# Seven of GpSimd's 392 gathers become single-row fetches that SyncE issues from a loaded address

## The chip, the cores and the metric

The kernel runs on one core of one Trainium2 chip. Times are device microseconds (us) of one execution, and the lower the better. A core has TensorE (PE: matmuls, with PEld its weight loads), VectorE (DVE), ScalarE (ACT), GpSimd (POOL) and SyncE (SP), each with an instruction queue of its own. [...] Transfers are carried by 16 DMA engines, whichever queue issues them.

## What is computed

One graph layer with a pre-norm over 100000 nodes of 64 features and 25000 edges:

```
h = jnp.maximum(_layernorm(x, axis=-1), 0.0)
x_i = h[src]; x_j = h[dst]
z = jnp.concatenate([x_i, x_j, edge_attr_32], axis=-1)
e = jax.nn.sigmoid(z @ W_f + b_f) * jax.nn.softplus(z @ W_s + b_s)
message = jax.ops.segment_sum(e, src, num_segments=100000)
normed = (message - mean) * jax.lax.rsqrt(var + BN_EPS) * gamma + beta
out = x + h + normed
```

So 2 x 25000 rows of x, 256 bytes each, have to be fetched by index, and 25000 message rows have to be added to a table by index.

## The kernel before

The work has two stages. Stage one gathers, computes the messages, and adds them to the table `msgs` in HBM; beside that it normalises all nodes into `y_kept` (the first 19 groups of it are spilled to HBM). Stage two squares the table for its variance, scales it, adds `y` and writes the output. A barrier of all engines stands between the stages, at about 900 us.

**Groups.** An edge group is 4 tiles of 128 edges; there are 49 (n = 0 to 48). For each tile GpSimd issues two gathers of 128 rows (`c` = 0 for source, 1 for destination), so a group has 8 gathers into `xg[:, n % 6, 2 * j + c, :]`, a ring of six slots (`gather`, L371 to L381). After gather(n) GpSimd issues the four scatters of group n - 6 (`accumulate`, L383 to L394), which wait for that group's combined messages (`comb_copied`), its targets, and the landing of the scatters before. GpSimd's program is a flat list; gather(n) waits only until group n - 6 has been centred.

**The other engines** run a pipeline of steps, one step for each group. Step n of VectorE ends the messages of group n - 3 (L545), sums and centres 16 node rows per partition (L459, L450), then waits for the gathers of group n, sums them (L470) and centres them (L450), which frees the slot; it normalises the group before (L519), makes targets, adds the residual of the group before (L537, four parts, the last of which raises `y_done`), and ends with `softplus` (L512). ScalarE and TensorE take squares, turns, products and the combination of equal sources between these.

**SyncE** loads the plain inputs. After a start with constants and the zeroing of `msgs` it runs a loop of 7 rounds (it = 1 to 7), six groups a round (u = 0 to 5), and in each group `load` issues 512 KB of x (`load_nodes`, L297 to L306) and the edge attributes (L308 to L320). `load(Group(it, u))` waits for `y_done` of group 6 it + u - 3 and for `ea_turned`. Thus in the loop SyncE loads two groups ahead of VectorE. The loop and its neighbours are:

```
            with sp.Fori(1, ITERS) as it:
                for u in range(UNROLL):
                    load(Group(it, u))
            for u in range(GROUPS - LAST + SKEW):
                load(Group(ITERS, u))
```

Of the kernel before, what the change touches and what calls it, by code (L numbers as in the profile page):

```python
# [21 lines left out]
I32 = mybir.dt.int32  # L22
ALU = mybir.AluOpType
# [3 lines left out]
P = 128  # L27
NODES, EDGES, F, EF = 100000, 25000, 64, 32
EPS = 1e-5
TILES = 4  # L30
GATHERED = 2 * TILES
# [4 lines left out]
ALL_TILES = E_COLS + 1  # L36
# [5 lines left out]
UNROLL = 6  # L42
# [4 lines left out]
G_SLOTS = 6  # L47
# [2 lines left out]
ACC_LAG = 6  # L50
ZERO_PARTS = 16
DUMP = (TILES + 1) * P
assert ALL_TILES == TILES * GROUPS and ITERS * UNROLL == LAST and UNROLL % SLOTS == 0 and UNROLL % G_SLOTS == 0
assert 0 < LAST_ROWS < BULK
assert (SPILL + 1 + SKEW) % UNROLL == 0
# [58 lines left out]
def wait_group(eng, sem, g, per=1):  # L114

    if not g.known or g.n >= 0:
        eng.wait_ge(sem, per * (g.n + 1) if per > 1 else g.n + 1)
# [43 lines left out]
def stage_one(nc, sem, x, src, dst, ea, w_f, b_f, w_s, b_s, msgs, y_spill,  # L161
              x_rows, ea_tiles, m_rows, y_kept, ones, ident, eps_col, one_col, msg_sum):
    with ExitStack() as ctx:
        def sb(name, shape, dt=F32):
            return ctx.enter_context(nc.sbuf_tensor(name, shape, dt))
# [1 line left out]
        def ps(name, shape):  # L167
            return ctx.enter_context(nc.psum_tensor(name, shape, F32))

        ids = sb("ids", [P, 2, ALL_TILES], I32)  # L170
        src_f = sb("src_f", [P, ALL_TILES])
        dump_row = sb("dump_row", [P, TILES])
        small = sb("small", [P, 4])
# [15 lines left out]
        xg = sb("xg", [P, G_SLOTS, GATHERED, F])  # L189
# [38 lines left out]
        prep = sem("prep")  # L228
# [2 lines left out]
        x_loaded = [sem(f"x_loaded{i}") for i in range(SLOTS)]  # L231
        ea_loaded = [sem(f"ea_loaded{i}") for i in range(SLOTS)]
        gathered = [sem(f"gathered{i}") for i in range(G_SLOTS)]
        own_staged = sem("own_staged")
        nodes_summed = sem("nodes_summed")
        edges_summed = sem("edges_summed")
        centred = sem("centred")
# [37 lines left out]
        def _(sp):  # L275
# [20 lines left out]
            def load_nodes(g):  # L296
                slot = g.slot(SLOTS)  # L297
                wait_group(sp, y_done, g.back(SLOTS))
                if g.known and g.n == STEPS - 1:
                    sp.dma_start(xn[:, slot, 0:LAST_ROWS, :],  # L300
                                 x_rows[:, BULK * LAST:N_ROWS, :]).then_inc(x_loaded[slot], 16)
                    sp.dma_start(xn[0:N_REST, slot, LAST_ROWS, :],
                                 x[P * N_ROWS:NODES, :]).then_inc(x_loaded[slot], 16)
                else:
                    sp.dma_start(xn[:, slot, :, :],
                                 x_rows[:, bass.ds((g.n - SKEW) * BULK, BULK), :]).then_inc(x_loaded[slot], 16)  # L306

            def load_edges(g):  # L308
                slot = g.slot(SLOTS)
                wait_group(sp, ea_turned, g.back(SLOTS))  # L310
                if g.known and g.n == LAST:
                    sp.dma_start(eas[:, slot, 0:TILES - 1, :],
                                 ea_tiles[:, E_COLS - TILES + 1:E_COLS, :]).then_inc(ea_loaded[slot], 16)
                    sp.dma_start(eas[0:E_REST, slot, TILES - 1, :],
                                 ea[P * E_COLS:EDGES, :]).then_inc(ea_loaded[slot], 16)
                    sp.dma_start(eas[E_REST:P, slot, TILES - 1, :],
                                 ea[0:P - E_REST, :]).then_inc(ea_loaded[slot], 16)
                else:
                    sp.dma_start(eas[:, slot, :, :],
                                 ea_tiles[:, bass.ds(g.n * TILES, TILES), :]).then_inc(ea_loaded[slot], 16)  # L320

            def load(g):
                if g.nodes():
                    load_nodes(g)
                if g.exists():
                    load_edges(g)
# [3 lines left out]
            def zero_table(u):  # L330
# [5 lines left out]
                if u == ZERO_PARTS - 1:  # L336
                    sp.dma_start(m_rows[:, whole:N_ROWS, :],
                                  zeros[:, 0:(N_ROWS - whole) * F].rearrange("p (r f) -> p r f", f=F)
                                  ).then_inc(table_zeroed, 16)
                    over = (N_REST + DUMP) // 96  # L340
                    sp.dma_start(msgs[P * N_ROWS:NODES + DUMP, :].rearrange("(p r) f -> p (r f)", p=96),
                                  zeros[0:96, 0:over * F]).then_inc(table_zeroed, 16)
# [5 lines left out]
            for u in range(SLOTS, UNROLL + 1):  # L348
                end = ZERO_PARTS * (u - 1) // (UNROLL - 1) if u < UNROLL else ZERO_PARTS
                for k in range(done, end):  # L350
                    zero_table(k)
                done = end
                if u < UNROLL:
                    load(Group(0, u))
            with sp.Fori(1, ITERS) as it:
                for u in range(UNROLL):
                    load(Group(it, u))
            for u in range(GROUPS - LAST + SKEW):
                load(Group(ITERS, u))

        @block.gpsimd
        def _(pool):
            pool.sem_inc(slots_free, UNROLL - 1)

            pool.memset(ident[:, :], 0.0).then_inc(masks_set, 1)
            pool.memset(upto[:, :], 1.0).then_inc(masks_set, 1)
            pool.wait_ge(masks_set, 2)
            pool.affine_select(out=ident[:, :], in_=ident[:, :], compare_op=ALU.not_equal, fill=1.0,
                               base=0, pattern=[[-1, P]], channel_multiplier=1).then_inc(masks_made, 1)
            pool.affine_select(out=upto[:, :], in_=upto[:, :], compare_op=ALU.is_ge, fill=0.0,  # L370
                               base=0, pattern=[[-1, P]], channel_multiplier=1).then_inc(masks_made, 1)  # L371

            def gather(n):
                if n >= G_SLOTS:
                    pool.wait_ge(centred, n - G_SLOTS + 1)
                for j in range(TILES):
                    for c in range(2):
                        pool.indirect_dma_start(  # L378
                            xg[:, n % G_SLOTS, 2 * j + c, :], None, x,
                            bass.IndirectOffsetOnAxis(ap=ids[:, c, n * TILES + j:n * TILES + j + 1], axis=0),  # L380
                        ).then_inc(gathered[n % G_SLOTS], 16)  # L381

            def accumulate(n):  # L383
                pool.wait_ge(comb_copied, n + 1)
                pool.wait_ge(target_done, n + 1)

                if n:
                    pool.wait_ge(accumulated, 16 * TILES * n)
                pool.sem_inc(slots_free, 1)
                for j in range(TILES):  # L390
                    pool.indirect_dma_start(  # L391
                        msgs, bass.IndirectOffsetOnAxis(ap=target[:, n % UNROLL, j:j + 1], axis=0),
                        comb[:, n % UNROLL, j, :], None, compute_op=ALU.add,
                    ).then_inc(accumulated, 16)  # L394

            pool.wait_ge(ids_loaded, 96)
            for n in range(GROUPS + ACC_LAG):
                if n < GROUPS:
                    gather(n)
                if n == ACC_LAG:  # L400
                    pool.wait_ge(table_zeroed, 16 * (ZERO_PARTS + 2))
                if n >= ACC_LAG:
                    accumulate(n - ACC_LAG)
            pool.wait_ge(accumulated, 16 * ALL_TILES)

        @block.vector
        def _(dve):
            dve.memset(zeros[:, :], 0.0).then_inc(zeros_set, 1)
            dve.memset(w_e[:, :, :], 0.0).then_inc(w_cleared, 1)
            dve.wait_ge(ids_loaded, 96)  # L410
            dve.memset(ones[:, :], 1.0)
            dve.memset(one_col[:, :], 1.0)
# [7 lines left out]

            dve.tensor_scalar(small[:, 1:2], small[:, 0:1], float(E_REST) + 0.5, None, ALU.is_lt)
            dve.tensor_scalar(small[:, 2:3], small[:, 0:1], float(NODES + TILES * P - 1), None, ALU.add)
            dve.tensor_copy(src_f[:, :], ids[:, 0, :]).then_inc(prep, 1)
            dve.wait_ge(prep, 2)
            dve.tensor_scalar(real[:, :], ones[:, :], small[:, 1:2], None, ALU.mult)
            dve.tensor_tensor(small[:, 3:4], src_f[:, E_COLS:ALL_TILES], small[:, 2:3],
# [21 lines left out]
            def less_mean(g, rows, x_of):  # L448
                n = rows.stop - rows.start
                return dve.scalar_tensor_tensor(  # L450
                    out=xc[:, g.slot(2), rows, :], in0=row_sum[:, rows].unsqueeze(2).to_broadcast([P, n, F]),
                    scalar=-1.0 / F, in1=x_of, op0=ALU.mult, op1=ALU.add)
# [12 lines left out]

            def centre_edges(g):
                slot, rows = g.slot(G_SLOTS), slice(0, GATHERED)
                dve.wait_ge(gathered[slot], 16 * GATHERED * g.uses(G_SLOTS) + 16 * GATHERED)
                wait_group(dve, centred, g.back(1))
                dve.tensor_reduce(row_sum[:, rows], xg[:, slot, :, :], AX.X, ALU.add).then_inc(edges_summed, 1)  # L470
                wait_group(dve, edges_summed, g)
                wait_group(dve, z_turned, g.back(2))
                less_mean(g, rows, xg[:, slot, :, :]).then_inc(centred, 1)

            def sum_squares(g):
                wait_group(dve, squared, g)
# [614 lines left out]
```

## Time and profile before

| | us |
|---|---|
| time, median of 3 runs (lowest, highest) | 1121.86 (1121.76, 1122.15) |
| the profiled execution: its own time | 1120.95 |
| its span in the trace | 1119.0 |
| busy: GpSimd, VectorE, TensorE, ScalarE | 684.3, 712.6, 703.5, 487.6 |
| stage one, up to the first load of stage two | 900.5 |

The span is 1.95 us shorter than the time of the same execution. Indices of lines are those of the kernel before. SyncE computes nothing, and its rows show when it issues transfers ("SPq"). Where a row has a bracket, it holds the time for which the engine stood idle before the instruction, and what ended that.

### The profile page before, as it was taken

The page shows a single profiled execution, that of the slowest core. Times are in us where ns is not written, and L with a number is a line of the kernel's source. Part 1 is how long each engine was busy: PE and PEld are TensorE (multiplying, and loading weights), DVE is VectorE, ACT ScalarE, POOL GpSimd, SP SyncE. Part 2 cuts the span into 40 slices and gives each one's busy share as a digit, 9 for nine tenths or more (in the row PEclk, how much of TensorE's full clock was granted, in tenths as well). Part 3 has the DMA queues.
Part 4 walks back from the last instruction along what each step waited for, and adds up shares of the span by engine and source line. Part 5 has one row for each costly group of instructions (what it writes and reads, how often), then busy time and mean ns, then how long its engine had stood idle before and what let it go on. Part 6 is the DMA issues. An engine that isn't in the chain of part 4 may idle for free. (4 is left out here: it accounts for less than half of the span.)

```text
span 1119.0 us, 11417 instructions
## 1 busy us (share of the span) xinstructions
PE 703.5 (63%) x2864; PEld 483.6 (43%) x2864; DVE 712.6 (64%) x1427; ACT 487.6 (44%) x1118; POOL 684.3 (61%) x596
## 2 busy tenths in 40 slices
PE   0675667566655665566566665765666246699986
PEld 0454445344543544355444544543455146433331
DVE  3475756657575665756656676575758545689956
ACT  0464555455554545545455554555547134300000
POOL 6755777778777787787877778777776610000000
PEclk9865555665565556655565565556556578989978
DMA  6995434344343432323233232332324289569998
GB/s 240 377 399 152 84 81 103 61 103 80 85 102 62 103 67 59 65 43 66 43 66 64 44 65 43 67 56 52 64 41 67 13 325 397 210 237 398 427 427 356
DMA packets 78295, 162.10 MB, mean 145 GB/s; under 512 B 39755, under 2 KB 46251, under 8 KB 69675
## 3 DMA queue, kind: packets, MB, share of 16 engines
q1 hardware_dynamic: 29947, 106.80, 26.3%
q0 software_dynamic: 40768, 19.31, 15.8%
q10 hardware_dynamic: 7536, 35.56, 7.8%
q14 instruction: 35, 0.29, 0.1%
q8 instruction: 9, 0.15, 0.1%
HBM read 93.87 MB, written 67.75 MB: 144 GB/s over the span
## 5 line engine op out<-in xcount | busy, mean ns | idle before, releaser
L378 POOL DMA_INDIRECT xg<-in_x_dram,ids x392 | 375.8, 959 | 122.2 <-issue 114.0
L391 POOL DMA_INDIRECT msgs_dram<-comb,target x196 | 307.4, 1568 | 91.1 <-issue 57.6
L470 DVE TENSOR_REDUCE row_sum<-xg 128x8 f32<-128x512 f32 x49 | 34.0, 694 | 263.2 <-DMA xg<-in_x_dram,ids 263.2
L768 PE MATMUL bank_c<-msg,same 128*128 128x64 f32 x980 | 185.7, 373 | 6.1 <-ACT same L666 6.1
L768 PEld LDWEIGHTS bank_c<-msg,same 128*128 128x128 f32 x980 | 180.4, 285 | 6.6 <-ACT same L666 6.5
L743 PE MATMUL ps_z<-ident,xc 128*128 128x128 f32 x196 | 53.0, 424 | 192.0 <-DVE xc L519 192.0
L743 PEld LDWEIGHTS ps_z<-ident,xc 128*128 128x128 f32 x196 | 34.7, 212 | 223.4 <-DVE xc L519 190.2
L620 ACT ACTIVATE sq<-xc 128x1536 f32<-128x1536 f32 (+2 forms) x53 | 73.4, 1385 | 118.1 <-DVE xc L450 118.1
L757 PEld LDWEIGHTS ps_v<-w_z,z_t 128*128 128x128 f32 x392 | 93.6, 327 | 50.0 <-issue 50.0
L966 PE MATMUL ps_all<-y_kept,ident 128*128 128x512 f32 x196 | 103.8, 670 | 13.3 <-DMA y_kept<-y_spill_dram 11.3
L666 ACT ACTIVATE same<-same,one_col 128x512 f32<-128x512 f32 x196 | 107.6, 550 | 1.6
L755 PE MATMUL ps_v<-w_e,ea_t 128*128 128x512 f32 x98 | 100.5, 1128 | 0.0
L757 PE MATMUL ps_v<-w_z,z_t 128*128 128x128 f32 x392 | 90.6, 411 | 0.0
L479 DVE TENSOR_REDUCE row_ssq<-sq 128x24 f32<-128x1536 f32 (+2 forms) x53 | 86.0, 1622 | 3.4 <-ACT sq L620 3.4
L519 DVE SCALAR_TENSOR_TENSOR xc<-xc,row_rstd 128x1536 f32<-128x1536 f32 (+2 forms) x53 | 86.1, 1624 | 1.5 <-ACT row_rstd L631 1.5
L660 ACT ACTIVATE same<-ps_src,own 128x512 f32<-128x512 f32 x196 | 86.6, 524 | 0.0
L735 PE MATMUL ps_src<-ident_b,own_b 128*128 128x128 bf16 x392 | 40.6, 265 | 72.6 <-ACT same L666 72.6
L673 ACT ACTIVATE comb<-bank_c 128x256 f32<-128x256 f32 x49 | 18.8, 384 | 151.0 <-PE ps_sum L771 145.8
L537 DVE TENSOR_TENSOR y_kept<-xc,xn 128x256 f32 (+1 forms) x196 | 81.7, 421 | 0.1
L947 PE MATMUL ps_all<-m_buf 128*128 128x128 f32 x304 | 44.6, 305 | 50.9 <-DMA m_buf<-msgs_dram 50.9
L1056 DVE TENSOR_TENSOR m_buf<-m_buf,scale 128x2048 f32<-128x2048 f32 (+3 forms) x33 | 57.1, 1730 | 17.0 <-DMA m_buf<-msgs_dram 16.9
L459 DVE TENSOR_REDUCE row_sum<-xn 128x16 f32<-128x1024 f32 x49 | 59.5, 1214 | 12.4 <-DMA xn<-in_x_dram 10.7
(106 smaller groups left out, 957.4 us busy)
## 6 DMA issues: line engine op xcount, KB each, us to landing
m_buf<-msgs_dram SPq DMA_DIRECT2D x38, 1024.0 KB, 20.8
msgs_dram<-zeros SPq DMA_DIRECT2D x16, 1536.0 KB, 17.5
xn<-in_x_dram SPq DMA_DIRECT2D x48, 512.0 KB, 3.7
out_dram<-m_buf ACTq DMA_DIRECT2D x20, 1024.0 KB, 9.7
y_spill_dram<-y_kept ACTq DMA_DIRECT2D x19, 512.0 KB
y_kept<-y_spill_dram SPq DMA_DIRECT2D x9, 1024.0 KB, 30.7
xg<-in_x_dram,ids POOLq DMA_INDIRECT x392
msgs_dram<-comb,target POOLq DMA_INDIRECT x196, 3.2
```

What stands on the lines that cost most here:

```text
L378: pool.indirect_dma_start(xg[:, n % G_SLOTS, 2 * j + c, :], None, x, bass.IndirectOffsetOnAxis(ap=ids[:, c, n * TILES + j:n * TILES + j + ...
L391: pool.indirect_dma_start(msgs, bass.IndirectOffsetOnAxis(ap=target[:, n % UNROLL, j:j + 1], axis=0), comb[:, n % UNROLL, j, :], None, com ...
L479: dve.tensor_reduce(row_ssq[:, rows], sq[:, rows, :], AX.X, ALU.add).then_inc(ssq_done, 1)
L519: dve.scalar_tensor_tensor(out=h, in0=h, scalar=0.0, in1=row_rstd[:, rows].unsqueeze(2) .to_broadcast([P, g.end_row - g.first_row, F]), op ...
L537: ins = dve.tensor_tensor(y_kept[:, bass.ds(row, n), :], xc[:, g.slot(2), rows, :], xn[:, g.slot(SLOTS), of_x, :], ALU.add)
L660: ins = act.activation(same[:, b, b:TILES, :], ps_src[:, b:TILES, :], ACT.Abs, scale=-1.0, bias=own[:, g.slot(UNROLL), b:b + 1])
L666: ins = act.activation(same[:, b, b:TILES, :], same[:, b, b:TILES, :], ACT.Relu, scale=-1.0, bias=one_col[:, 0:1], accum_out=matches[:, b: ...
L743: ins = pe.transpose(ps_z[:, j, :], xc[:, g.slot(2), 2 * j:2 * j + 2, :].rearrange("p c f -> p (c f)"), ident[:, :])
L755: pe.matmul(v[:, :, :], ea_t[:, :], w_e[:, :, :], start=False, stop=True, skip_group_check=True)
L757: ins = pe.matmul(v[:, j, :], z_t[:, j, :], w_z[:, :], start=False, stop=True, skip_group_check=True)
L768: pe.matmul(ps_c[:, j, :], same[:, b, j, :], msg[:, b, :], start=(b == 0), stop=(b == j))
L966: pe.matmul(ps_y[k % 2][:, c:c + w, :], ident[:, :], y_of(order[i])[:, r + c:r + c + w, :], start=True, stop=False, skip_group_check=True)
```

## The change

One gather in a round is no longer issued by GpSimd: the last destination gather (j = 3, c = 1) of groups 9, 15, 21, 27, 33, 39 and 45. SyncE fetches those 128 rows instead. For each row p it loads one 32-bit number, `row_at[p]`, from SBUF into a register, and issues a DMA of 64 floats from x at that offset into partition p of slot 3. The rows of a round are issued in five pieces (25, 26, 25, 26 and 26 rows), each behind the `load` of u = 0 to 4. VectorE writes `row_at` (index times 64) for the next round once it has centred group 6 it + 3, and raises `rows_wanted`; a round of SyncE starts with a wait on that. Before it sums group 6 it + 3, VectorE waits for seven gathers and for all 128 rows (`rows_loaded`).

```diff
@@ stage_one, SyncE
+            x_flat = x.rearrange("n f -> (n f)")
+
+            def load_rows(rows):
+                for p in rows:
+                    at = sp.value_load(row_at[p:p + 1, 0:1])
+                    sp.dma_start(xg[p:p + 1, ROW_GROUP, GATHERED - 1, :],
+                                 x_flat[bass.ds(at, F)].unsqueeze(0)).then_inc(rows_loaded, 16)
+
             with sp.Fori(1, ITERS) as it:
                 for u in range(UNROLL):
+                    if u == 0:
+                        sp.wait_ge(rows_wanted, it)
                     load(Group(it, u))
+                    if u < ROW_STEPS:
+                        load_rows(range(P * u // ROW_STEPS, P * (u + 1) // ROW_STEPS))
@@ stage_one, GpSimd
+            def by_rows(n):
+                return n >= UNROLL and n % UNROLL == ROW_GROUP
+
             def gather(n):
                 if n >= G_SLOTS:
                     pool.wait_ge(centred, n - G_SLOTS + 1)
                 for j in range(TILES):
-                    for c in range(2):
+                    for c in range(1 if by_rows(n) and j == TILES - 1 else 2):
@@ stage_one, VectorE
+            dve.memset(ids[:, :, ALL_TILES:], 0)
@@ centre_edges(g)
-                dve.wait_ge(gathered[slot], 16 * GATHERED * g.uses(G_SLOTS) + 16 * GATHERED)
+                by_rows = g.off % UNROLL == ROW_GROUP
+                dve.wait_ge(gathered[slot], 16 * (GATHERED - by_rows) * g.uses(G_SLOTS) + 16 * GATHERED)
+                if by_rows and not (g.known and g.n < UNROLL):
+                    dve.wait_ge(rows_loaded, 16 * P * g.it)
...
+                if by_rows:
+                    wait_group(dve, centred, g)
+                    dve.tensor_scalar(row_at[:, :], ids[:, 1, bass.ds((g.n + UNROLL) * TILES + TILES - 1, 1)],
+                                      float(F), None, ALU.mult).then_inc(rows_wanted, 1)
```

ROW_GROUP is 3 and ROW_STEPS is 5; `ids` is 24 columns wider, and those are cleared.

**SyncE, start of its loop.** Before, one round begins like this (xn is a slot of x, eas one of the edge attributes; the rows marked ISA carry the waits):

```order
L355 ISA
L305 ISA [waits y_done]
L305 DMA xn<-in_x_dram 128x1024
L319 ISA [waits ea_turned]
L319 DMA eas<-in_edge_attr_dram 128x128
L117 REGISTER_ALU
L305 ISA [waits y_done]
```

With the change the same place reads:

```order
L119 ISA [waits rows_wanted]
L310 ISA [waits y_done]
L310 DMA xn<-in_x_dram 128x1024
L324 ISA [waits ea_turned]
L324 DMA eas<-in_edge_attr_dram 128x128
L365 TENSOR_LOAD row_at
L366 REGISTER_ALU
L366 DMA xg<-in_x_dram 1x64
```

The wait on the addresses is new at the top, and the last three rows repeat, 25 times behind this load and 128 times in the round; the next pair of loads stands behind them.

**GpSimd, around one of the seven groups.** Before, in the flat list of gathers (L378) and scatters (L391):

```order
L378 DMA xg<-in_x_dram,ids 128x64 x7
L391 DMA msgs_dram<-comb,target 100640x64 [waits accumulated,comb_copied,target_done]
L391 DMA msgs_dram<-comb,target 100640x64 x3
L378 DMA xg<-in_x_dram,ids 128x64 [waits centred]
L378 DMA xg<-in_x_dram,ids 128x64 x7
```

With the change:

```order
L399 DMA xg<-in_x_dram,ids 128x64 x7
L412 DMA msgs_dram<-comb,target 100640x64 [waits accumulated,comb_copied,target_done]
L412 DMA msgs_dram<-comb,target 100640x64 x3
L399 DMA xg<-in_x_dram,ids 128x64 [waits centred]
L399 DMA xg<-in_x_dram,ids 128x64 x6
```

The group fetched by rows has one gather less (1 + 6 for 1 + 7); the scatters behind it follow directly. The group ahead of it is as it was.

**VectorE, step of such a group.** With the change these rows stand where it sums and centres the gathered rows (before, the wait for eight gathers and the two instructions on xg alone):

```order
L493 REGISTER_ALU [waits gathered3]
L495 TENSOR_REDUCE row_sum<-xg 128x8 [waits centred,rows_loaded]
L472 SCALAR_TENSOR_TENSOR xc<-row_sum,xg 128x512 [waits z_turned,edges_summed]
L501 ISA [waits centred]
L501 TENSOR_SCALAR row_at<-ids 128x1
L548 SCALAR_TENSOR_TENSOR xc<-xc,row_rstd 128x1536 [waits rstd_done]
```

The wait for the rows stands ahead of the sum, and the new addresses are made behind the centring.

## Rows read from the trace of the kernel before

**Rows 1.** Costliest groups: count, busy us, mean ns, idle before them and releaser

```profile
L378 POOL DMA_INDIRECT xg<-in_x_dram,ids x392 | 375.8, 959 | 122.2 <-issue 114.0
L391 POOL DMA_INDIRECT msgs_dram<-comb,target x196 | 307.4, 1568 | 91.1 <-issue 57.6
L470 DVE TENSOR_REDUCE row_sum<-xg 128x8 f32<-128x512 f32 x49 | 34.0, 694 | 263.2 <-DMA xg<-in_x_dram,ids 263.2
```

**Rows 2.** Timeline of GpSimd: start us, us, instruction

```profile
299.43 0.95 POOL L378 DMA_INDIRECT xg<-in_x_dram,ids  x1 [0.30 <-issue]
300.68 0.94 POOL L378 DMA_INDIRECT xg<-in_x_dram,ids  x1 [0.30 <-issue]
...
311.94 1.02 POOL L378 DMA_INDIRECT xg<-in_x_dram,ids  x1 [0.30 <-issue]
...
329.54 1.01 POOL L378 DMA_INDIRECT xg<-in_x_dram,ids  x1 [0.30 <-issue]
```

**Rows 3.** Timeline of GpSimd: the last four scatters of stage one

```profile
891.45 1.54 POOL L391 DMA_INDIRECT msgs_dram<-comb,target  x1 [2.53 <-DMA msgs_dram<-comb,target]
...
896.99 1.54 POOL L391 DMA_INDIRECT msgs_dram<-comb,target  x1 [0.30 <-issue]
```

**Rows 4.** Timeline of SyncE: first row of its loop, then an ordinary group

```profile
77.23 0.92 SPq L305 DMA_DIRECT2D xn<-in_x_dram  x1
...
311.93 0.33 SPq L305 DMA_DIRECT2D xn<-in_x_dram  x1
312.46 0.33 SPq L319 DMA_DIRECT2D eas<-in_edge_attr_dram  x1
329.54 0.33 SPq L305 DMA_DIRECT2D xn<-in_x_dram  x1
```

**Rows 5.** Line 305 alone, durations in ns: minimum/median/maximum

```profile
L305 SPq DMA_DIRECT2D xn<-in_x_dram x48: 327/333/922, 41.6 to 850.9; - x48
L305 SPq FUSED_REGOPS  x42: 52/52/67, 77.1 to 787.7; - x42
L305 SPq MOVE xn<-in_x_dram x42: 29/29/37, 77.2 to 787.8; - x42
```

**Rows 6.** Timeline of SyncE: small transfers at the start

```profile
1.73 0.29 SPq L283 DMA_DIRECT2D ids<-in_src_dram  x1
2.07 0.36 SPq L278 DMA_DIRECT2D ids<-in_dst_dram  x1
...
3.84 0.59 SPq L290 DMA_DIRECT2D w_z<-in_L_gnn_W_f_dram  x1
...
6.49 0.30 SPq L293 DMA_DIRECT2D b_row<-in_L_gnn_b_f_dram  x1
6.84 0.47 SPq L289 DMA_DIRECT2D w_z<-in_L_gnn_W_s_dram  x1
```

**Rows 7.** DMA issues: count, KB each, median us to landing

```profile
xn<-in_x_dram SPq DMA_DIRECT2D x48, 512.0 KB, 3.7
out_dram<-m_rest ACTq DMA_DIRECT2D x1, 8.0 KB, 1.6
```

**Rows 8.** Timeline of VectorE: sums of gathered rows, residual, targets

```profile
305.60 0.69 DVE L470 TENSOR_REDUCE row_sum<-xg 128x8 f32<-128x512 f32 x1 [5.62 <-DMA xg<-in_x_dram,ids]
...
308.60 0.16 DVE L496 TENSOR_TENSOR later<-matches,no_later 128x4 f32<-128x4 f32 x1
...
323.22 0.69 DVE L470 TENSOR_REDUCE row_sum<-xg 128x8 f32<-128x512 f32 x1 [5.71 <-DMA xg<-in_x_dram,ids]
...
781.55 0.69 DVE L470 TENSOR_REDUCE row_sum<-xg 128x8 f32<-128x512 f32 x1 [5.49 <-DMA xg<-in_x_dram,ids]
...
834.44 0.69 DVE L470 TENSOR_REDUCE row_sum<-xg 128x8 f32<-128x512 f32 x1 [5.95 <-DMA xg<-in_x_dram,ids]
...
846.06 1.75 DVE L519 SCALAR_TENSOR_TENSOR xc<-xc,row_rstd 128x1536 f32<-128x1536 f32 x1
```

**Rows 9.** Timeline of TensorE: two successive turns of z at the end

```profile
837.58 1.12 PE L743 MATMUL ps_z<-ident,xc 128*128 128x128 f32 x4 [3.29 <-DVE xc L519]
...
851.71 1.06 PE L743 MATMUL ps_z<-ident,xc 128*128 128x128 f32 x4
```

**Rows 10.** Timeline: last combined copy, VectorE's last instruction, first load of stage two

```profile
873.67 0.38 ACT L673 ACTIVATE comb<-bank_c 128x256 f32<-128x256 f32 x1 [5.27 <-PE ps_sum L774]
...
885.56 0.42 DVE L607 TENSOR_REDUCE msg_sum<-ps_sum 128x64 f32<-128x256 f32 x1
...
900.46 4.50 SPq L909 DMA_DIRECT2D m_buf<-msgs_dram  x9
```

More of the change, by code:

```diff
@@ L52 @@
 DUMP = (TILES + 1) * P
+ROW_GROUP = 3
+ROW_STEPS = 5
 assert ALL_TILES == TILES * GROUPS and ITERS * UNROLL == LAST and UNROLL % SLOTS == 0 and UNROLL % G_SLOTS == 0
@@ L168, in ps @@
             return ctx.enter_context(nc.psum_tensor(name, shape, F32))
-        ids = sb("ids", [P, 2, ALL_TILES], I32)
+        ids = sb("ids", [P, 2, ALL_TILES + UNROLL * TILES], I32)
+        row_at = sb("row_at", [P, 1], I32)
         src_f = sb("src_f", [P, ALL_TILES])
@@ L233, in stage_one @@
         gathered = [sem(f"gathered{i}") for i in range(G_SLOTS)]
+        rows_wanted = sem("rows_wanted")
+        rows_loaded = sem("rows_loaded")
         own_staged = sem("own_staged")
@@ L422, in _ @@
             dve.tensor_scalar(small[:, 2:3], small[:, 0:1], float(NODES + TILES * P - 1), None, ALU.add)
-            dve.tensor_copy(src_f[:, :], ids[:, 0, :]).then_inc(prep, 1)
+            dve.tensor_copy(src_f[:, :], ids[:, 0, 0:ALL_TILES]).then_inc(prep, 1)
             dve.wait_ge(prep, 2)
```

## The prediction, made before the change was run

> **What bounds the kernel now.** I read the costliest groups first. GpSimd has 392 gathers and 196 scatters, and the idle time before them is almost all "issue", while VectorE stands 263.2 us before the sum of the gathered rows, released by the gathers [rows 1]. So in stage one the others wait for GpSimd. Its timeline says the same: a gather starts 1.25 us after the one before (0.95 busy, 0.30 issue), and a whole group of eight gathers and four scatters repeats every 17.60 us, 311.94 to 329.54 [rows 2]; VectorE's sums of gathered rows follow at the same distance, 305.60 to 323.22, each with 5.5 to 5.9 us of idle time before it [rows 8]. The end of stage one is GpSimd's too: its last scatter ends at 898.53 and stage two's first load is issued at 900.46 [rows 3, 10]. VectorE was done at 885.98 [rows 10]. Stage two is not touched, so everything is decided by when stage one ends: 900.5 now.
>
> **What the change removes.** Seven gathers at 1.25 us [rows 2] are 8.75 us of GpSimd's own path. If nothing else came late, the stage would end at 891.7, and VectorE's 885.98 would still be covered. That is the most that can be won.
>
> **What it adds on VectorE.** Eight multiplications of one column, nearest row 0.16 us (the 128x4 operation at 308.60), and a wait on the centring just done. They stand ahead of the normalisation in a step with 5.6 us idle [rows 8]: nothing. The wider `ids` costs one small clear at the start, under the idle time there. The wait for the 128 rows is the part that counts.
>
> **What it adds on SyncE: the price of a row.** A round now has 128 times load a register, register arithmetic, DMA issue. None of these overlaps another, because one queue executes them in order. I call their sum c.
> - The issue: a DMA with a computed address takes 0.333 us [rows 5]; small ones at the start take 0.29 and 0.30, and their successors start 0.34 and 0.35 us after them, so the gap is 0.04 to 0.05 [rows 6]. I take 0.32 and 0.04.
> - The arithmetic for such an address: 0.052 for the fused operation and 0.029 for the move that stands with each computed address [rows 5].
> - The register load from SBUF is in no row. Below, it can't be less than the move, 0.029. [...] The nearest rows are SyncE's other memory operations, its DMA issues: the cheapest is 0.29, the slowest that is no pile-up is 0.59 [rows 6]. I take the cheapest, 0.29, because a single number is moved, and keep 0.03 and 0.59 as ends.
>
> So c is 0.29 + 0.05 + 0.03 + 0.32 + 0.04 = 0.73 us, with ends 0.47 and 1.03.
>
> [...]
>
> **Why 128 c is not simply compared with a round.** A round of six groups has 6 x 17.6 - 1.25 = 104.4 us. 128 x 0.73 is 93.4, which seems to fit. But SyncE cannot spread that over the whole round, since its chain closes on itself:
> 1. `load` for u = 0 waits for `y_done` of the group that has just been fetched by rows. Then come five loads and 128 rows. One load is 0.86 us, 311.93 to 312.79 [rows 4], five are 4.3.
> 2. The last row lands about 2 us later (8 KB took 1.6, 512 KB took 3.7 [rows 7]).
> 3. Only then can VectorE sum group 6 it + 3. `y_done` of that group comes at the end of the next step. When nothing else is late, a step takes about 12 us: 834.44 to 846.06 is 11.6 on VectorE, 837.58 to 851.71 is 14.1 on TensorE at its slowest, and 17.62 less the idle 5.7 is 11.9 [rows 8, 9]. From a sum to SyncE's next load of x are 6.3 us, 305.60 to 311.93 [rows 4, 8]. Together 18.3.
>
> A round therefore can't be shorter than R = 128 c + 4.3 + 2 + 18.3 = 128 c + 24.6. It exceeds 104.4 from c = 0.62. With 0.73 it is 118.0, 13.6 us more than GpSimd needs.
>
> **What covers this, and for how long.** GpSimd is ahead: it gathers until six groups are out, and scatters group n - 6 behind gather(n). A late step n delays the scatters of group n - 2, which GpSimd reaches some four groups later (70 us; less about 16 us for the way from the sum to the combined copy). So some 54 us of delay are absorbed before GpSimd stands, and VectorE wins back 5.6 us in each step that is not held. That hides the delay in the middle, but not at the end: group 45 is the last fetched by rows, and all that follows it has to be done.
>
> **The sum.** The loop starts at 77.2 [rows 4]. Seven rounds: the rows of group 45 have landed at 77.2 + 6 R + 128 c + 6.3. From that sum three steps of 12 lead to group 48's; from there VectorE needs 51.5 us to its last instruction (834.44 to 885.98 [rows 8, 10]): 88 in all. GpSimd's way is 36 + 39.6 (834.44 to 874.05, the last combined copy) + 7.1 (last four scatters) + 1.9 = 84.6 [rows 3, 8, 10], a little less. The stage ends at 77.2 + 6 (128 c + 24.6) + 128 c + 6.3 + 88 = 319 + 896 c. For c = 0.73 that is 973; group 45 is summed at 885 instead of 781.55 [rows 8]. Against 900.5 the stage is 73 us longer. The profiled execution's own 1120.95 becomes 1194; the median lies 0.9 above it: **1195 us**.
>
> The formula is steep: 0.01 us more for a row is 9 us more for the kernel. It breaks even at c = 0.649, that is a load of 0.21 us, and the whole gain is there below c = 0.639.
>
> **Rival one, faster.** If the register load costs 0.19 us or less (six moves [rows 5]), the rows stay behind GpSimd's work: in the first round group 9's rows land at 77.2 + 81 + 6 = 164 against some 147 (781.55 less 36 steps of 17.62), 17 us late, in the others they are a few us late, and the 54 us cover it. Then only the seven gathers count: 1121.9 - 8.7 = 1113 us. For it: a load moves four bytes inside the core, and the issue may be nearer to 0.29 than to 0.32. [...] Chance 0.26.
>
> **Rival two, the load is as dear as SyncE's slowest issue.** 0.5 to 0.59 us gives c = 0.94 to 1.03 and a stage end at 1161 to 1242: 1383 to 1463 us. Now even 128 c is more than a round, and GpSimd stands for most of the difference. It needs only that reading memory from the queue costs more than telling a DMA to. Chance 0.18.
>
> **Rival three, they cancel.** c between 0.64 and 0.652: within 0.2% of before, 1122 us. The band is narrow: 0.05. The middle case, c from 0.652 to 0.94, has 0.51.
>
> **Numbers.** The likeliest case has its own range, 1130 to 1300. The range for 8 in 10 has to reach the faster rival and leaves out the upper part of rival two: 1111 to 1400. About 0.2% is what a measurement of this kernel can tell from no change. Faster 0.26, same 0.05, slower 0.69.
>
> **What the changed profile would show.** The register load has its own rows: their duration is the term that decides. c is the distance of two row fetches on SyncE. If I am right, the sum of groups 9, 15, ... 45 waits for the rows by DMA and not for gathers, these sums stand 118 us apart instead of 105.7, the five steps after them have no idle time before L470's sum until VectorE has caught up, GpSimd begins to wait for the combined copy from the fourth or fifth round on, and stage two starts near 973. I would be wrong if a row costs under 0.64 us; if SyncE's issues pile up because small fetches land slowly one after another, which would add to c; or if a step of VectorE without waits is much shorter than 12 us, which moves R by as much.

## The result, and the profile after the change

The changed kernel takes 1430.00 us (median of 4 runs, 1425.68 to 1431.41) against 1122.01 before (1121.76 to 1123.00): a ratio of 1.274, with a 95% interval of 1.271 to 1.277. It is 308 us slower. The forecast said 1195 and a range up to 1400; the direction held, the size did not.

The page of the changed kernel, its groups in the same columns as [rows 1], and two of its DMA queues:

```profile
span 1429.7 us, 15031 instructions
L412 POOL DMA_INDIRECT msgs_dram<-comb,target x196 | 309.2, 1577 | 403.6 <-issue 355.1
L399 POOL DMA_INDIRECT xg<-in_x_dram,ids x385 | 369.7, 960 | 120.0 <-issue 110.6
L495 DVE TENSOR_REDUCE row_sum<-xg 128x8 f32<-128x512 f32 x49 | 33.6, 685 | 359.4 <-DMA xg<-in_x_dram 330.2
...
q14 instruction: 81, 0.66, 0.2%
```

GpSimd does its work in the same time as before (a gather 960 ns against 959), seven gathers fewer. But the idle time before its scatters has grown from 91.1 to 403.6 us, and most of VectorE's wait before the sum is now put down to `in_x_dram` alone: these are SyncE's row fetches (a GpSimd gather would read `in_x_dram,ids`). They are 330.2 of the 359.4 us, in seven waits. VectorE also stands 223.4 us before the sum of its node rows (L481), where it stood 12.4 before: the plain loads of x now queue behind pieces of rows on SyncE. That wait sets nothing by itself, since SyncE is issuing rows all through it.

The rows of the two lines of a row fetch on SyncE (L365 and L366), durations in ns (minimum/median/maximum):

```profile
L365 SPq TENSOR_LOAD <-row_at x896: 434/501/1808, 79.6 to 1118.3; - x180
L366 SPq ALU_OP  x896: 32/33/52, 80.8 to 1118.8; - x180
L366 SPq MOVE xg<-in_x_dram x896: 29/29/38, 80.9 to 1118.9; - x180
L366 SPq DMA_DIRECT2D xg<-in_x_dram x896: 254/258/298, 81.0 to 1119.0; - x180
```

This is the number that was in no row of before: one register load costs 0.501 us. The four instructions add up to 0.821 us, and they run one after another (of one row the load starts at 945.6, the arithmetic at 946.1, the move and the DMA at 946.2). SyncE's timeline of one round shows what a row costs with the gaps between them (start us, length us, and the count of DMAs merged):

```profile
945.26 24.46 SPq L366 DMA_DIRECT2D xg<-in_x_dram  x26
977.49 0.36 SPq L310 DMA_DIRECT2D xn<-in_x_dram  x1
978.06 0.36 SPq L324 DMA_DIRECT2D eas<-in_edge_attr_dram  x1
989.25 0.34 SPq L310 DMA_DIRECT2D xn<-in_x_dram  x1
989.80 0.33 SPq L324 DMA_DIRECT2D eas<-in_edge_attr_dram  x1
990.82 23.84 SPq L366 DMA_DIRECT2D xg<-in_x_dram  x25
```

26 rows take 24.46 us from the first DMA's start to the last one's end: (24.46 - 0.26) / 25 = 0.97 us a row. So c is 0.97, where I had 0.73. The last row of that round was issued by 969.72, and VectorE's sum began at 970.82, 1.1 us later; 18.4 us after that sum SyncE got its next load of x out (989.25).

VectorE's sums at L495, which stood 105.7 us apart per round before:

```profile
821.22 0.70 DVE L495 TENSOR_REDUCE row_sum<-xg 128x8 f32<-128x512 f32 x1 [47.25 <-DMA xg<-in_x_dram]
833.33 0.68 DVE L495 TENSOR_REDUCE row_sum<-xg 128x8 f32<-128x512 f32 x1
846.39 0.68 DVE L495 TENSOR_REDUCE row_sum<-xg 128x8 f32<-128x512 f32 x1
...
970.82 0.69 DVE L495 TENSOR_REDUCE row_sum<-xg 128x8 f32<-128x512 f32 x1 [47.39 <-DMA xg<-in_x_dram]
...
1120.16 0.69 DVE L495 TENSOR_REDUCE row_sum<-xg 128x8 f32<-128x512 f32 x1 [46.93 <-DMA xg<-in_x_dram]
```

The sum of a group fetched by rows waits 47 us for them, the next one follows 12.1 us later without waiting for a gather, and a round is (1120.16 - 216.75) / 6 = 150.6 us long on average (152.4 at first, 149.3 at last). Stage two's first load starts at 1208.86, 308.4 us later than before [rows 10]: of the 310.7 us between the two profiled spans, all but 2.3 lie in stage one.

### The profile page after: what moved, and what is told of

It is laid out like the page before. It is cut to its first block and busy times, and to the rows that moved or that the text cites. A ratio compares the mean times of both kernels' runs of the same rounds, so it can differ in the third digit from the quotient of the medians.

```text
span 1429.7 us, 15031 instructions
## 1 busy us (share of the span) xinstructions
PE 673.0 (47%) x2864; PEld 466.1 (33%) x2864; DVE 711.3 (50%) x1436; ACT 481.2 (34%) x1118; POOL 680.0 (48%) x589
## 5 line engine op out<-in xcount | busy, mean ns | idle before, releaser
L412 POOL DMA_INDIRECT msgs_dram<-comb,target x196 | 309.2, 1577 | 403.6 <-issue 355.1
L399 POOL DMA_INDIRECT xg<-in_x_dram,ids x385 | 369.7, 960 | 120.0 <-issue 110.6
L772 PE MATMUL ps_z<-ident,xc 128*128 128x128 f32 x196 | 48.5, 396 | 548.6 <-DVE xc L548 548.6
L495 DVE TENSOR_REDUCE row_sum<-xg 128x8 f32<-128x512 f32 x49 | 33.6, 685 | 359.4 <-DMA xg<-in_x_dram 330.2
L797 PE MATMUL bank_c<-msg,same 128*128 128x64 f32 x980 | 172.0, 353 | 5.9 <-ACT same L695 5.7
L481 DVE TENSOR_REDUCE row_sum<-xn 128x16 f32<-128x1024 f32 x49 | 59.9, 1222 | 223.4 <-DMA xn<-in_x_dram 223.4
L797 PEld LDWEIGHTS bank_c<-msg,same 128*128 128x128 f32 x980 | 167.1, 267 | 7.0 <-ACT same L695 6.4
L784 PE MATMUL ps_v<-w_e,ea_t 128*128 128x512 f32 x98 | 93.8, 1057 | 0.0
L514 DVE SCALAR_TENSOR_TENSOR not_later<-ps_src,own,upto 128x128 f32<-128x128 f32 x196 | 67.1, 346 | 0.0
L1088 DVE TENSOR_TENSOR m_buf<-m_buf,ps_all 128x2048 f32<-128x2048 f32 (+3 forms) x33 | 57.2, 1732 | 13.6 <-PE ps_all L1003 12.1
```

The costliest lines, as they stand in the source:

```text
L399: pool.indirect_dma_start(xg[:, n % G_SLOTS, 2 * j + c, :], None, x, bass.IndirectOffsetOnAxis(ap=ids[:, c, n * TILES + j:n * TILES + j + ...
L412: pool.indirect_dma_start(msgs, bass.IndirectOffsetOnAxis(ap=target[:, n % UNROLL, j:j + 1], axis=0), comb[:, n % UNROLL, j, :], None, com ...
L772: ins = pe.transpose(ps_z[:, j, :], xc[:, g.slot(2), 2 * j:2 * j + 2, :].rearrange("p c f -> p (c f)"), ident[:, :])
L784: pe.matmul(v[:, :, :], ea_t[:, :], w_e[:, :, :], start=False, stop=True, skip_group_check=True)
L797: pe.matmul(ps_c[:, j, :], same[:, b, j, :], msg[:, b, :], start=(b == 0), stop=(b == j))
```

## Experiments

The theory was by then: a row costs 0.97 us because each has its own register load, and a round lasts (rows x 0.97 + 24.6) us because the chain of SyncE and VectorE closes on itself. The rivals: small fetches land slowly or pile up; the row path has a fixed cost; SyncE's own work alone sets the round; the price is paid per register and not per load.

**1. Without the register load.** The rows come from fixed addresses:

```diff
-                    at = sp.value_load(row_at[p:p + 1, 0:1])
                     sp.dma_start(xg[p:p + 1, ROW_GROUP, GATHERED - 1, :],
-                                 x_flat[bass.ds(at, F)].unsqueeze(0)).then_inc(rows_loaded, 16)
+                                 x_flat[p * F:(p + 1) * F].unsqueeze(0)).then_inc(rows_loaded, 16)
```

> The changed kernel without the register load: each of the 128 DMAs of a round fetches a row at a fixed address (row p of x), so the values of those rows are others. Seven gathers are still off GpSimd, all waits stand. Theory (the register load is the price): a row costs 0.95 us less 0.50 for the load and 0.03 for the arithmetic, about 0.4 us, so a round of SyncE is 128 x 0.4 + 25 = 76 us, under GpSimd's 104.4, and the time is 1122 - 8.7 = 1113 us. Rival A (small fetches land slowly or pile up in the DMA engines): a round stays well over 104 us and the time over 1200 us. Rival B (taking a gather from GpSimd is worth nothing, something else sets its pace): 1122 us.

Measured: 1114.83 us (1111.59 to 1118.51) where before took 1123.41 on the same chip; ratio 0.992 (0.990 to 0.995). All 896 small fetches and all waits are there, and the 315 us are gone. SyncE's timeline in that kernel:

```profile
449.22 0.37 SPq L310 DMA_DIRECT2D xn<-in_x_dram  x1
449.79 0.37 SPq L324 DMA_DIRECT2D eas<-in_edge_attr_dram  x1
450.19 7.75 SPq L365 DMA_DIRECT2D xg<-in_x_dram  x26
466.22 0.37 SPq L310 DMA_DIRECT2D xn<-in_x_dram  x1
```

26 rows take 7.75 us, 0.30 each, and SyncE then waits until 466.22. So rival A falls: the fetches themselves neither pile up nor land late. These are the same 128 addresses in each round; experiment 4 has the real ones. Rival B falls too: seven gathers less are worth 8.6 us, as 7 x 1.25 says.

**2 and 3. Fewer rows, each with its load.** The number of rows in a round was cut to 64 and to 96:

```diff
-                        load_rows(range(P * u // ROW_STEPS, P * (u + 1) // ROW_STEPS))
+                        load_rows(range(96 * u // ROW_STEPS, 96 * (u + 1) // ROW_STEPS))
...
-                    dve.wait_ge(rows_loaded, 16 * P * g.it)
+                    dve.wait_ge(rows_loaded, 16 * 96 * g.it)
```

> The changed kernel with 64 of the 128 rows fetched in a round (13 or so in each piece); the other 64 partitions keep what was in the slot, so their values are others. Loads of registers are kept for the rows that are fetched. Theory (round = rows x 0.97 + 24.6): 64 x 0.97 + 24.6 = 86.7 us, under 104.4: 1113 us. Rival A, a fixed cost of the row path beside the price of a row (waiting on registers, code fetch): over 1130 us.

Measured: 1116.14 us (1114.33 to 1117.34), ratio 0.993 (0.990 to 0.995). That is 3 us above the forecast and 14 below the rival's 1130: no fixed cost of the row path shows.

> The changed kernel with 96 of the 128 rows fetched in a round; the other 32 partitions keep what was in the slot. Theory (the chain closes on itself, round = rows x 0.97 + 24.6): 117.7 us a round, 13 us over GpSimd's 104.4; stage one ends at 77.2 + 6 x 117.7 + 93 + 6.3 + 88 = 971 us, time 1192 us, and group 45 is summed near 883 us. Rival (only SyncE's own work counts, round = rows x 0.97 + 5): 98 us, which is under 104.4: 1113 us.

Measured: 1212.07 us (1210.54 to 1213.66), ratio 1.079 (1.077 to 1.081). With 96 rows SyncE is busy for some 98 us of a round (96 x 0.97 + 5), less than GpSimd's 104.4, and yet the kernel is 90 us slower than with 64. SyncE's work alone doesn't say that; the closed chain does. The sums of groups 9 and 45 in that kernel:

```profile
185.31 0.69 DVE L495 TENSOR_REDUCE row_sum<-xg 128x8 f32<-128x512 f32 x1 [35.14 <-DMA xg<-in_x_dram]
...
902.53 0.69 DVE L495 TENSOR_REDUCE row_sum<-xg 128x8 f32<-128x512 f32 x1 [34.55 <-DMA xg<-in_x_dram]
```

A round is (902.53 - 185.31) / 6 = 119.5 us, where the formula gives 117.7; the first sum is 9 us late against its 176.5. Together these are the 20 us that the forecast of 1192 missed. The last three rounds are 118.5 us each, 0.8 from the formula.

**4. Eight indices in one register load.** The 128 indices of a round lie on one partition, SyncE fetches them itself during the round before, and VectorE writes no addresses:

```diff
+            ahead = UNROLL * TILES
+            dst_tiles = dst[ahead:ahead + P * E_COLS].rearrange("(p t) -> t p", p=P)
+            def load_ids(it):
+                col = it * ahead + (ROW_GROUP * TILES + TILES - 1)
+                sp.dma_start(row_at[0:1, :], dst_tiles[bass.ds(col, 1), :],
...
-                for p in rows:
-                    at = sp.value_load(row_at[p:p + 1, 0:1])
-                    sp.dma_start(xg[p:p + 1, ROW_GROUP, GATHERED - 1, :],
-                                 x_flat[bass.ds(at, F)].unsqueeze(0)).then_inc(rows_loaded, 16)
+                for p0 in rows:
+                    _, ats = nc.values_load_multi_w_load_instructions(
+                        row_at[0:1, p0:p0 + ROW_LOAD], engines=[mybir.EngineType.SP])
+                    for p, at in enumerate(ats, p0):
+                        sp.dma_start(xg[p:p + 1, ROW_GROUP, GATHERED - 1, :],
+                                     x[bass.ds(at, 1), :]).then_inc(rows_loaded, 16)
```

> All 128 rows, computing the reference's output: the 128 indices of a round lie on one partition (SyncE fetches them from dst at the end of the round before), and one register load brings 8 of them; SyncE multiplies by 64 in its address arithmetic. 16 loads in a round instead of 128. VectorE no longer writes addresses. Theory (most of the 0.50 us is paid once for each load): a row costs 0.45 + 0.5 to 0.8 divided by 8, that is 0.51 to 0.55 us, a round 90 to 95 us, under 104.4: 1113 us. Rival (the price is per register): 0.95 us a row, a round of 147 us, 1400 us or more.

Measured: 1113.72 us (1111.75 to 1114.47), ratio 0.991 (0.988 to 0.993). It fetches the same rows as the changed kernel, and it is 0.9% faster than the kernel before. Its load and a piece of 24 rows:

```profile
L374 SPq TENSOR_LOAD <-row_at x112: 714/781/2179, 91.8 to 772.5; - x112
...
451.34 11.81 SPq L377 DMA_DIRECT2D xg<-in_x_dram  x24
...
464.12 0.70 DVE L509 TENSOR_REDUCE row_sum<-xg 128x8 f32<-128x512 f32 x1 [9.04 <-DMA xg<-in_x_dram]
```

A load of eight costs 0.781 us where a load of one costs 0.501: each further one 0.04. A row is (11.81 - 0.23) / 23 = 0.50 us, and the rows landed before 464.12, 9 us after VectorE was ready for them. VectorE's wait is then inside what GpSimd absorbs: the last three rounds are 104.4 to 104.8 us, which is GpSimd's own time for a round.

**5 and 6. The same work, begun earlier.** The first piece of a round was moved ahead of the load of u = 0, so that it needs only the new addresses. First with 96 rows, then with all 128 (nothing waits for `rows_begun`):

```diff
                     if u == 0:
                         sp.wait_ge(rows_wanted, it)
+                        sp.sem_inc(rows_begun, 1)
+                        load_rows(range(0, 96 // ROW_STEPS))
                     load(Group(it, u))
-                    if u < ROW_STEPS:
+                    if 0 < u < ROW_STEPS:
```

> As the run with 96 rows (the other 32 partitions keep what was in the slot), but the first piece of a round (19 rows) stands ahead of the load of u = 0, behind the wait for the new addresses alone. SyncE then begins when it has issued the load of u = 5, about 7 us after the sum of the group fetched by rows, and not 18 us after it. Theory (the chain closes on itself): a round falls by about 11 us, from 119.8 to 108, near GpSimd's 104.4; time about 1135 us (1125 to 1150), against 1212 with the load in front. Rival (SyncE's work or the DMA engines set the round): as many instructions as before, 1212 us.

Measured: 1172.39 us (1167.29 to 1173.38), ratio 1.044 (1.041 to 1.047).

> The changed kernel with all 128 rows, computing the reference's output; the first piece of a round (25 rows) stands ahead of the load of u = 0, as in the run before. Theory: every round after the first falls by about 11 us of 150.6, so 6 x 11 = 66 us: about 1362 us. Rival: 1430 us, as nothing is removed.

Measured: 1390.06 us (1386.16 to 1391.41), ratio 1.240 (1.237 to 1.243).

Both fell by 40 us with the same number of loads, fetches and waits, which SyncE's work alone can't explain. But both missed their forecasts, by 37 and 28 us, and fell by little more than half of the 11 us a round that I had expected: a round became 113.6 us (from 119.5) and 144.1 us (from 150.6). The rows of the first show where the rest stayed. VectorE's sum and its new addresses, then SyncE's load of u = 5 and its next piece of rows:

```profile
527.66 0.69 DVE L498 TENSOR_REDUCE row_sum<-xg 128x8 f32<-128x512 f32 x1 [34.80 <-DMA xg<-in_x_dram]
...
529.26 0.15 DVE L504 TENSOR_SCALAR row_at<-ids 128x1 int32 x1 [0.18 <-DVE xc L475]
...
534.89 0.36 SPq L325 DMA_DIRECT2D eas<-in_edge_attr_dram  x1
539.62 18.24 SPq L367 DMA_DIRECT2D xg<-in_x_dram  x19
```

The addresses are there from 529.41, SyncE is done with the load at 535.25, and the first row's DMA starts at 539.62. The row's own register load and arithmetic explain 0.6 us of these 4.4. Most of the others pass at the loop's end, between the branch and the instruction after it. In the same round (line 370):

```profile
L370 SPq COMPARE_BRANCH  x1: 45/45/45, 535.4 to 535.4; - x1
L370 SPq MOVE  x1: 34/34/34, 538.9 to 538.9; - x1
```

and in the kernel before (line 355):

```profile
L355 SPq COMPARE_BRANCH  x1: 45/45/45, 683.2 to 683.2; - x1
L355 SPq FUSED_REGOPS  x1: 50/50/50, 683.4 to 683.4; - x1
```

After this branch 3.5 us pass before the next instruction (3.8 in the changed kernel, 978.5 to 982.3), after that of the short loop 0.2. The change made a round of the loop some 500 instructions longer (15031 - 11417 in seven rounds), and the DMA queue that the page calls "instruction" has 81 packets instead of the 35 on the page of before:

```profile
q14 instruction: 35, 0.29, 0.1%
```

The runs between these two show a step. In experiment 1 a round is 132 instructions longer than before, the branch costs 0.2 to 0.3 us and the queue has 36 packets; in experiment 2 it is 260 longer, with 3.5 to 3.7 us and 67 packets. So the gap and the packets both rise between 132 and 260 instructions more; what the engine does in the gap is in no row, and no run separates one cost of a long loop from another. In the changed kernel this time lies under SyncE's wait for `y_done` (978.42 to 989.25 above) and costs nothing; moved forward, it became visible. With it the account closes: SyncE now begins 11.3 us after the sum and not 18.4, and the last three rounds of experiment 5 are 112.6 us or less, 6 to 7 below the 118.5 of experiment 3.

**7. Control: one index in each load.** Experiment 4's kernel with 128 loads of one in place of 16 loads of eight; the only edit is the number:

```diff
-ROW_LOAD = 8
+ROW_LOAD = 1
```

> Control for the version with 8 indices per load, computing the reference's output: the same source of the indices (one partition, fetched by SyncE), the same address arithmetic, but one register load for each index, 128 in a round. Theory (the number of loads decides): a row costs about 0.93 us, a round 144 us, time about 1390 us (1370 to 1430). Rival (the gain of that version came from leaving VectorE out, or from where the indices lie): near 1114 us.

Measured: 1438.13 us (1436.99 to 1441.05), ratio 1.283 (1.280 to 1.287). The size was missed by 48 us (I took 0.93 us for a row, but its rounds are 151.0 us, as the changed kernel's are; and its first load of x in the loop is issued at 90.96 instead of 77.52, behind the fetch of the first indices). The verdict is clear: neither the place of the indices nor VectorE's part made experiment 4 fast. The number of loads did.

**8. Sixteen indices in each load.** The same edit, with 16.

> 16 indices per register load, 8 loads in a round, computing the reference's output. One load took 0.50 us and one of 8 took 0.78, so 16 should take about 1.1 us, 0.07 a row, and a row about 0.48 us. GpSimd is the bound either way: theory 0.991 of before, the same as with 8 (1113 to 1115 us on a chip where before takes 1122 to 1123). Rival (rows that come earlier still help): under 1110 us.

Measured: 1115.12 us (1108.93 to 1117.45), ratio 0.993 (0.991 to 0.996). The load took:

```profile
L374 SPq TENSOR_LOAD <-row_at x56: 1162/1181/1502, 91.5 to 761.3; - x56
```

1.181 us for 16, so 0.07 a row. VectorE's waits before these sums fell from 9 to 4.7 us in the later rounds and the time did not move beyond its interval. The last four rounds are 104.4 us each: GpSimd is the bound again.

## Why the prediction was wrong in size

**The step that failed is the price of a row, c.** The sum had 0.29 for the load, 0.08 for arithmetic and move, 0.32 for the issue and 0.04 for a gap: 0.73. Measured are 0.50, 0.06, 0.26 and some 0.15 for gaps: 0.97. The load was mis-sized by 0.21 and the gaps by 0.11: I counted one gap for a row, and there are four instructions, which at 0.04 each would make 0.16. The issue was 0.06 cheaper, the arithmetic 0.02. I had put the load at SyncE's cheapest DMA issue because only one number is moved. Nothing supported that choice beyond nearness: it was an estimate from the rows of another operation. Why the load takes longer than an issue (0.50 against 0.26) no run tests. At about 9 us for each 0.01, these 0.24 us are some 215 us.

**The rival that had it right** was the second one, a load as dear as SyncE's slowest issue (0.5 to 0.59, 1383 to 1463 us), to which I gave 0.18. The range ended at 1400 and so left out most of a case that I had priced. This case's rows: 0.434 at the least and 0.501 in the middle for one number, and 0.04 to 0.05 for each further one on a contiguous row (0.781 for 8, 1.181 for 16).

**The closed chain was right.** R = 128 c + 24.6 gives 148.8 us with c = 0.97; 150.6 were measured. Its parts: from a sum to SyncE's next load of x 18.4 us (18.3 forecast), the landing 1.1 (2 forecast), a step without waits 12.1 (12 forecast). A pair of loads in the round was put at 0.86 us and costs some 1.2 (in the last round the first row of a piece starts 2.1 us after the last row of the piece before has started, 1.2 more than the distance of two rows). Experiments 3, 5 and 6 show the closure by itself.

**The tail was right.** From the sum of group 45 to stage two are 1208.86 - 1120.16 = 88.7 us; 88 were forecast. The formula 319 + 896 c gives 1188 for c = 0.97. The 21 us to 1208.9 are the first round, whose sum came at 216.75 instead of 207.7 (its first 25 rows took 29.24 us instead of some 24, beside the last of the zeroing of `msgs`; the cause was not tested), and six rounds that were 1.8 us longer each. VectorE is the last to end, as forecast: its last instruction ends at 1208.50, GpSimd's last scatter at 1204.50.

**What GpSimd absorbs was put at the wrong place.** I had named the combined copy and 54 us. The first round in the changed kernel shows another wait ending last. VectorE's sum of group 9, its targets, and GpSimd's first scatter after that:

```profile
216.75 0.69 DVE L495 TENSOR_REDUCE row_sum<-xg 128x8 f32<-128x512 f32 x1 [47.32 <-DMA xg<-in_x_dram]
...
220.60 0.16 DVE L535 TENSOR_TENSOR target<-moved,own 128x4 int32<-128x4 f32 x1
...
221.57 1.61 POOL L412 DMA_INDIRECT msgs_dram<-comb,target  x1 [23.35 <-issue]
```

The scatter starts 0.8 us after the targets are written (220.76 and 221.57), which are those of the group three steps back. The trace calls this wait "issue", so it has to be read from the times. The sum was some 71 us late (216.75 against 146: 781.55 of [rows 8] less 36 steps of 17.62 and one gather) and GpSimd stood 23, so it had absorbed 47 or 48 us. GpSimd first waits in the first round, where I had said the fourth or fifth. That comes from c: 71 us are more than 54, too. The forecast did not follow from its own numbers either: with c = 0.73 the first sum is some 31 us late and each round adds 13.6, so 54 us are used up in the third. The end is not moved by the cover: it hangs on the chain and the tail alone.

**Parts that were right.** The gain of the seven gathers: 8.6, 7.3, 9.7 and 6.8 us in experiments 1, 2, 4 and 8, 8.75 forecast. VectorE's address row took 0.15 us and stood under idle time. Stage two took 220.8 us in the profiled execution, against 218.5 before.

## What to carry to other kernels

When work is moved to an idle queue, price every instruction that one item needs there, with a gap behind each (here four instructions of 0.82 us together, and 0.15 us of gaps), and don't price a register load by a DMA issue (here 0.50 against 0.26 us). If one item costs too much, load several at once: 128 loads of one and 16 loads of eight differ here by 324 us (experiments 7 and 4). Then look for the wait that closes the helper's chain on its own result: what counts is not the helper's work in a round but that work plus the way back to its next start. While that sum stayed below GpSimd's 104.4 us it cost nothing here (experiments 1, 2, 4 and 8); above it a round took about as long as the sum (119.5 us for 117.7 in experiment 3, 150.6 for 148.8 in the changed kernel).

## What the runs showed of the hardware

- One 32-bit number from SBUF into a register of SyncE: 0.501 us (0.434 at the least; 0.493 where the numbers lie on one partition). Eight contiguous ones in one instruction: 0.781 us. Sixteen: 1.181 us.
- Issuing a DMA of one 256-byte row: 0.258 us in the kernels that load one index for each row, 0.228 in those that load eight or sixteen, 0.252 at fixed addresses (medians). At fixed addresses rows followed each other at 0.30 us, and 128 of them in a round cost nothing that could be measured: the kernel was 8.6 us faster, as its seven gathers less account for.
- From the branch back to the start of SyncE's loop to the next instruction: 0.2 to 0.3 us in the loop of before and in one with 132 instructions more (experiment 1), 3.5 to 3.7 with 260 more (experiment 2), 3.6 to 3.9 with some 500 more (the changed kernel).
